# Weights split in the context half, odd tiles interpolated in another bank, and eleven blocks with an order of their own on each engine

## The chip, the cores and the metric

The kernel runs on one core of a Trainium2 chip (trn2). Its time is the device time of that core in microseconds; smaller is better. Four instruction queues matter here: TensorE (PE), VectorE (DVE), ScalarE (ACT) and GpSimd (POOL). Each runs its own list in order. They meet only in semaphores. SyncE (SP) issues most transfers.

## The reference, cut to what matters

Two layers, each a cross attention and a small expert network, over 2048 tokens of 256 numbers and a context of 1601 rows. The change lies in the second layer:

```python
x = x + _L1_xattn_ref(_layernorm(x), ctx_1024, ...)
x = x + _L1_ffn_ref(_layernorm(x), gate_W, expert_W, out_W)

# _L1_xattn_ref(char_emb = tokens, subword_emb = context)
char2sub = softmax(Q_char @ K_sub.T * scale) @ V_sub        # one row for each token
sub2char = softmax(Q_sub @ K_char.T * scale) @ V_char       # one row for each context row
sub2char = _interp_linear(sub2char, L_char)                 # 1601 rows stretched to 2048
gate = sigmoid(concat([char2sub, sub2char]) @ Wg.T + bg)
out = gate * char2sub + (1 - gate) * sub2char

# _L1_ffn_ref: eight logits, their softmax, p > 0.3 counted; what is left of the experts is two products
h = einsum('nd,ehd->neh', x, expert_W); final = einsum('neh,ne->nh', h, scale); out = final @ out_W.T
```

## The kernel before, in words

All of the second layer is one function, `cross_phase`. Its score blocks are numbered n = 0 to 111. Blocks 0 to 55 are the context half: groups 0 to 5 of context rows attend to the tokens and give `sub2char`. Group 5 has blocks 40 to 55; they are narrower in keys (one key tile each, three row tiles). Blocks 56 to 111 are the cross half: groups 6 to 13, seven blocks each, two token tiles per group, attending to the 1601 context rows. The last block of each group has one key tile, the others two.

A block n passes through the engines so: PE `score` (some blocks ahead), ACT `evacuate` (L2342), DVE `maximum` (L2693, L2696), then once per group the maxima are turned on PE (`max_turn`, L2093), reduced on DVE (`tops`, L2706), spread on ACT (`spread_max`, L2352) and turned back on PE (`spread_turn`, L2100). Then DVE `subtract` (L2717), ACT `exponent` (L2357) and `high` (L2364), DVE `low` (L2722), PE `weighted` (L2118 to L2120). High and low are the two float32r parts of a float32 number; each product is three matmuls (`mm3`, L43 to L45).

When a group closes, DVE `finish` (L2733, L2747) writes `c2s` for its two tiles, the even one u and the odd one v = u + 1. Each tile then goes through a closing chain over the blocks of the groups after it. In words, with lines: POOL `tents_of` makes the interpolation weights, PE `interpolate` (L2137, L2138) makes `sub2char` of the tile in a PSUM bank, ACT `copy` (L2399) keeps it in `inter`, POOL `mix` (L2599, L2600), PE `turn` (L2146), ACT `gate_high` (L2386), DVE `gate_low` (L2756), PE `gate`, DVE `bias` (L2763), ACT `squash` (L2390), DVE `move` (L2769, L2773) and `statistics` (L2779, L2782), POOL `inverse` (L2605 to L2609), ACT `normalise` (L2405), PE `x_turn` (L2166), `x_split` on ACT (L2376) and DVE (L2752), PE `first_products`, ACT `keep_first` (L2370), DVE and ACT `softly` and `soft_exponent` (L2797 to L2812, L2380), PE `second_product`, DVE `add` (L2820, L2825), SP store.

What sets the order is the loop `for n in range(NBLK)` on each engine: with b the block's place in its group (0 to 6), `closing_step`, `early_step`, `middle_step` and `late_step` hang one piece of the chain on each b. For the odd tile v, `interpolate(v)` stands at the end of b = 2 on PE, `copy(v)` at the start of b = 3 on ACT, and `turn(v)` on PE just behind `weighted` of b = 3. On ACT, `spread_max` of the next group stands at the end of b = 2, so ahead of `copy(v)`. Interpolation, turned tile and gate product share bank 0 (`jb`). After block 111 the rest of the chains of tiles 12 to 15 follows, in a list written by hand.

The closing weights (`late_weights`: expert 0, expert 1, Wg and the small gate matrix of the experts) are split into high and low by ACT (L2512) and DVE (L2936) at the ends of blocks 58, 59, 60 and 61.

## Time and profile before

| | |
|---|---|
| median of 3 runs | 1010.18 us (1009.96 to 1013.87) |
| the profiled execution, its own time | 1008.3 us |
| its span | 1006.4 us |
| PE busy | 940.8 us (93%) |
| DVE busy | 742.5 us (74%) |
| ACT busy | 584.8 us (58%) |
| POOL busy | 357.4 us (36%) |

The span runs from the first to the last instruction. Busy times are unions of instruction times. Matmuls overlap each other in a record, so PE reads as busy whenever it is fed. All times below are from the start of the span. On it the cross half's blocks run from about 746 us to 968 us, one group in some 28.5 us, and what remains of the closing chains runs from there to 1003.6 us.

### The profile page before, as it was taken

To read this page: it belongs to the slowest core of one execution; us is meant where nothing else is said; L and a number is where in the kernel's file an instruction comes from. 1 tells how busy PE (TensorE), PEld (TensorE's weight loads), DVE (VectorE), ACT (ScalarE), POOL (GpSimd) and SP (SyncE) were. 2 spreads that over 40 slices of the span, in tenths; PEclk is the share of its full clock that TensorE was granted. 3 is DMA by queue.
4 is the path that set the end of the run, shared out by engine and by line. 5 is a ranking of instruction groups with operands and counts; after the bars stand their busy time and mean duration, and the time that the engine had idled before them with its cause. 6 is when DMAs were issued, how large, how long until landed. Compare 5 with 4: busy or idle time off the path is not lost. (4 is left out here: it accounts for less than half of the span.)

```text
span 1006.4 us, 19300 instructions
## 1 busy us (share of the span) xinstructions
PE 940.8 (93%) x6934; PEld 885.3 (88%) x6934; DVE 742.5 (74%) x1704; ACT 584.8 (58%) x1243; POOL 357.4 (36%) x512
## 2 busy tenths in 40 slices
PE   8999999899899999999999999999996999999864
PEld 8899998588899999997788999999996989999764
DVE  7678777577687888865566677776588489898874
ACT  6356666432477777762345766665575466666431
POOL 4515555508334443315632000000026345544461
PEclk9999999999999999999999999999998999999987
DMA  8200000111588888824212000001000000000000
GB/s 239 84 1 1 1 1 1 42 44 63 185 262 265 266 259 253 262 95 129 63 42 85 1 1 2 1 2 43 1 22 2 1 12 22 20 14 23 21 22 21
DMA packets 50949, 72.38 MB, mean 72 GB/s; under 512 B 5489, under 2 KB 33777, under 8 KB 50865
## 3 DMA queue, kind: packets, MB, share of 16 engines
q1 hardware_dynamic: 45152, 55.81, 18.1%
q0 software_dynamic: 5024, 14.42, 4.2%
q8 instruction: 50, 0.82, 0.3%
q10 hardware_dynamic: 688, 1.05, 0.3%
q14 instruction: 35, 0.28, 0.1%
HBM read 59.34 MB, written 11.93 MB: 71 GB/s over the span
## 5 line engine op out<-in xcount | busy, mean ns | idle before, releaser
L2118 PE MATMUL wide<-V_hi,pt 128*128 128x258 f32 x400 | 117.7, 294 | 5.4 <-DVE pt L2722 5.4
L2120 PE MATMUL wide<-V_hi,pt 128*128 128x258 f32 x400 | 114.8, 287 | 0.0
L2119 PE MATMUL wide<-V_lo,pt 128*128 128x256 f32 x400 | 114.3, 286 | 0.0
L2118 PEld LDWEIGHTS wide<-V_hi,pt 128*128 128x128 f32 x400 | 77.3, 193 | 6.0 <-DVE pt L2722 5.8
L2579 POOL TENSOR_SCALAR V_hi<-rows 128x256 fp32r<-128x256 f32 (+1 forms) x9 | 8.9, 984 | 202.8 <-PE bank L2120 202.0
L2119 PEld LDWEIGHTS wide<-V_lo,pt 128*128 128x128 f32 x400 | 77.9, 195 | 0.2
L2120 PEld LDWEIGHTS wide<-V_hi,pt 128*128 128x128 f32 x400 | 77.5, 194 | 0.0
L43 PE MATMUL bank<-rx_hi,expert_w_hi 128*128 128x256 f32 x256 | 73.6, 287 | 1.6 <-PEq L1100 1.6
L45 PE MATMUL bank<-rx_hi,expert_w_lo 128*128 128x256 f32 x256 | 71.5, 279 | 0.0
L44 PE MATMUL bank<-rx_lo,expert_w_hi 128*128 128x256 f32 x256 | 71.5, 279 | 0.0
L503 POOL DMA_INDIRECT rxr<-token_rows,lists x39 | 56.8, 1457 | 27.6 <-issue 14.9
L43 PE MATMUL wide<-XT_hi,expert_w_hi 128*128 128x256 f32 (+1 forms) x216 | 63.8, 295 | 0.0
L44 PE MATMUL wide<-XT_lo,expert_w_hi 128*128 128x256 f32 (+1 forms) x216 | 62.3, 289 | 0.0
L45 PE MATMUL wide<-XT_hi,expert_w_lo 128*128 128x256 f32 (+1 forms) x216 | 62.3, 289 | 0.0
L514 DVE TENSOR_TENSOR expert_w_lo<-sraw,expert_w_hi 128x1024 fp32r<-128x1024 f32 x39 | 47.3, 1222 | 15.5 <-ACT expert_w_hi L510 15.4
L2696 DVE TENSOR_TENSOR rows<-rows,Fx 128x512 f32<-128x512 f32 (+2 forms) x60 | 40.7, 678 | 24.2 <-ACT Fx L2342 23.4
L1541 DVE TENSOR_TENSOR a0pt<-bank,a0pt 128x512 fp32r<-128x512 f32 x64 | 37.4, 584 | 28.0 <-ACT a0pt L1405 27.5
L1298 PE MATMUL bank<-a0pt,expert_w_hi 128*128 128x256 f32 x208 | 56.1, 300 | 1.4 <-issue 1.3
L43 PE MATMUL bank<-XT_hi,expert_w_hi 128*128 128x512 f32 x136 | 54.7, 402 | 1.5 <-PEq L1212 0.6
L43 PE MATMUL wide<-CT_hi,expert_w_hi 128*128 128x256 f32 (+1 forms) x192 | 55.2, 287 | 0.9 <-DVE XT_lo L2642 0.9
L45 PE MATMUL wide<-CT_hi,expert_w_lo 128*128 128x256 f32 (+1 forms) x192 | 54.8, 286 | 0.0
L44 PE MATMUL wide<-CT_lo,expert_w_hi 128*128 128x256 f32 (+1 forms) x192 | 54.8, 286 | 0.0
(527 smaller groups left out, 3639.6 us busy)
## 6 DMA issues: line engine op xcount, KB each, us to landing
sraw<-w1T SPq DMA_DIRECT2D x14, 512.0 KB, 4.6
sraw<-w3T SPq DMA_DIRECT2D x14, 512.0 KB, 4.9
sraw<-w2T SPq DMA_DIRECT2D x14, 512.0 KB, 5.0
raw_even<-w1T SPq DMA_DIRECT2D x11, 512.0 KB, 4.4
raw_even<-w3T SPq DMA_DIRECT2D x11, 512.0 KB, 5.0
raw_even<-w2T SPq DMA_DIRECT2D x11, 512.0 KB, 5.0
routed_results<-rys POOLq DMA_DIRECT2D x15, 256.0 KB, 4.5
X<-x SPq DMA_DIRECT2D x4, 512.0 KB, 6.6
```

The costliest lines, as they stand in the source:

```text
L43: pe.matmul(out, wh, xh, start=first, stop=False)
L44: pe.matmul(out, wh, xl, start=False, stop=False)
L45: return pe.matmul(out, wl, xh, start=False, stop=last)
L503: pool.indirect_dma_start(xr[:, j % 2, t, :], None, rows_in[:, :], bass.IndirectOffsetOnAxis(ap=lists[:, q:q + 1], axis=0))\
L514: dve.tensor_tensor(w_lo[:, par, piece(k)], raws[par][:, piece(k)], w_hi[:, par, piece(k)].bitcast(F32), ALU.subtract).then_inc(split_done ...
L1298: pe.matmul(ob[:, 0:2 * P], V_hi[:, k, :], both, start=k == 0, stop=False)
L1541: dve.tensor_tensor(weights(g, 1), transposed(g), weights(g, 0).bitcast(F32), ALU.subtract).then_inc(tlo, 1)
L2118: pe.matmul(dst[:, 0:D + 2], hi[:, x], v_hi(k), start=opens(n) and j == 0, stop=False)
L2119: pe.matmul(dst[:, 0:D], hi[:, x], v_lo(k), start=False, stop=False)
L2120: m = pe.matmul(dst[:, 0:D + 2], lo[:, x], v_hi(k), start=False, stop=closes(n) and k == keys_of(n)[-1])
L2579: pool.tensor_scalar(tent(i)[:, 0:n * P], d, 1.0, 0.0, ALU.add, ALU.max).then_inc(tent_done, 1)
L2696: dve.tensor_tensor(mx[:, 0:w], mx[:, 0:w], place(n), ALU.max).then_inc(maxed, 1)
```

## The change

Four things.

1. The closing weights are split at blocks 47, 48, 49 (expert 0, Wg, gate matrix) and 57 (expert 1), no longer at 58 to 61. Waits on `late_low` are renumbered.
2. Odd tiles are interpolated in bank 2 (`ib`), one block earlier: `interpolate(v)` at b = 1, `copy(v)` at b = 2.
3. POOL makes the tents four tiles ahead (before: two), and `inverse(i - 1)` comes behind `mix(i)`. Tokens 13 to 15 have places of their own and are fetched early. Several semaphores are split in two (`moved` into `scaled` and `moved`, `stat` into `stat` and `gathered`, `soft` into three).
4. The loops end at block 101 (`END_AT`). Blocks 101 to 111 and all that is left of tiles 9 to 15 follow as a written list for each engine. Tiles 13, 14 and 15 get banks of their own for gate and x work (`jb`, `xb`, `second_bank`), tile 15 its own gate inputs (`gin`), and tiles from 11 on two buffers `xn_of`.

```diff
+                LATE = [first[SG - 1] + 7, first[SG - 1] + 8, first[SG - 1] + 9, NSB + 1]
...
-                        if NSB + 2 <= n < NSB + 6:
-                            hi, lo, src = late_weights[n - NSB - 2]
+                        if n in LATE:
+                            hi, lo, src = late_weights[LATE.index(n)]
...
                 def jb(i):
-                    return score_bank[0] if i == LAST else banks[0]
+                    return score_bank[i - 13] if 13 <= i < LAST else banks[0]
 
                 def xb(i):
-                    return score_bank[1] if i == LAST else banks[1 + i % 2]
+                    return mb if i == 14 else banks[1] if i == LAST else banks[1 + i % 2]
+
+                def second_bank(i):
+                    return weighted_bank[i - 14] if i >= 14 else xb(i)
+
+                def ib(i):
+                    return jb(i) if i % 2 == 0 or i >= 13 else banks[2]
...
+                        elif i % 2 == 0:
+                            pe.wait_ge(biased, i)
+                        elif i > 4:
+                            pe.wait_ge(out_done, i - 3)
                         else:
-                            pe.wait_ge(biased, i)
+                            pe.wait_ge(finished, NC)
...
-                        if b == 2 and real(v):
+                        if b == 1 and real(v):
                             interpolate(v)
...
-                        if b == 3 and real(v):
+                        if b == 2 and real(v):
                             copy(v)
...
-                    tents_of(1)
-                    for i in range(NT):
+                    for i in range(1, 4):
+                        tents_of(i)
+                    for i in range(11):
                         mix(i)
-                        if real(i + 2):
-                            tents_of(i + 2)
-                        inverse(i)
+                        if i:
+                            inverse(i - 1)
+                        if i < 10:
+                            tents_of(i + 4)
...
-                    for n in range(NBLK):
+                    for n in range(END_AT):
...
+                    turn(11)
+                    weighted(END_AT)
+                    spread_turn(NG - 1)
+                    weighted(END_AT + 1)
+                    gate(11)
+                    weighted(END_AT + 2)
+                    first_products(9)
+                    weighted(END_AT + 3)
+                    interpolate(12)
+                    second_product(9)
+                    interpolate(13)
+                    x_turn(10)
+                    turn(12)
+                    weighted(END_AT + 4)
+                    turn(13)
+                    weighted(END_AT + 5)
+                    gate(12)
+                    weighted(END_AT + 6)
+                    first_products(10)
+                    weighted(END_AT + 7)
+                    gate(13)
+                    weighted(END_AT + 8)
+                    weighted(END_AT + 9)
+                    weighted(END_AT + 10)
+                    x_turn(11)
...
+                    gate(14)
+                    gate(15)
...
```

The lists of ACT, DVE and POOL are of the same kind. Three places show what moves.

First, DVE just behind the maxima of group 7 (L2706 is `tops`, L2936 the low part of a closing weight, L2696 a maximum, L2717 the subtractions for group 7, L2733 the first step of `finish` for tile 0). Before:

```order
L2706 TENSOR_REDUCE top<-bank 128x2
L2936 TENSOR_TENSOR expert_w_lo<-sraw,expert_w_hi 128x512
L2693 COPY rows<-Fx 128x512
L2722 TENSOR_TENSOR pt<-Fx,pt 128x256
L2936 TENSOR_TENSOR expert_w_lo<-sraw,expert_w_hi 128x1024
L2696 TENSOR_TENSOR rows<-rows,Fx 128x512
L2717 TENSOR_TENSOR Fx<-Fx,bank 128x512 x4
L2936 TENSOR_TENSOR expert_w_lo<-rt_raw,expert_w_hi 128x2x8
L2733 RECIPROCAL inverse_sum<-wide 128x1
```

The same place on DVE now (line numbers of the changed kernel: L2838 is `tops`, L2828 the maximum, L2849 the subtractions, L2865 the first step of `finish`):

```order
L2838 TENSOR_REDUCE top<-bank 128x2
L2825 COPY rows<-Fx 128x512
L2854 TENSOR_TENSOR pt<-Fx,pt 128x256
L2828 TENSOR_TENSOR rows<-rows,Fx 128x512
L2849 TENSOR_TENSOR Fx<-Fx,bank 128x512 x4
L2865 RECIPROCAL inverse_sum<-wide 128x1
```

Three splits are gone from between them; the fourth stays some rows ahead.

Second, PE at b = 2 of a group in the cross half, between the last score and `weighted` of b = 3 (L2166 is `x_turn`, L2137 and L2138 `interpolate` of the odd tile, L2093 `max_turn`, L2118 `weighted`). Before:

```order
L45 MATMUL wide<-XT_hi,expert_w_lo 128x256
L2166 MATMUL bank<-ident,sraw 128x128 x2
L2137 MATMUL bank<-CT_hi,V_lo 128x256
L2138 MATMUL bank<-CT_lo,V_lo 128x256
L2093 MATMUL bank<-ident,rows 128x128 x2
L2118 MATMUL wide<-V_hi,pt 128x258
```

Now (L2201 is `x_turn`, L2115 `max_turn`, L2140 `weighted`):

```order
L45 MATMUL wide<-XT_hi,expert_w_lo 128x256
L2201 MATMUL bank<-ident,sraw 128x128 x2
L2115 MATMUL bank<-ident,rows 128x128 x2
L2140 MATMUL wide<-V_hi,pt 128x258
```

The interpolation has gone up by one block, behind the even tile's gate product.

Third, DVE from the last `tops` on, where the written list begins. Before (L2752 is `x_split` of tile 9, L2756 `gate_low`, L2769 and L2773 `move`, L2717 `subtract` for group 13, L2722 `low`):

```order
L2706 TENSOR_REDUCE top<-bank 128x2
L2752 TENSOR_TENSOR XT_lo<-bank,XT_hi 128x2x128
L2722 TENSOR_TENSOR pt<-X,pt 128x512
L2756 TENSOR_TENSOR expert_w_lo<-bank,expert_w_hi 128x512
L2769 SCALAR_TENSOR_TENSOR sraw<-sraw 128x256
L2773 SCALAR_TENSOR_TENSOR X<-sraw,X 128x256
L2779 BN_STATS stats<-X 128x6
L2782 BN_AGGR MV<-stats 128x2
L2717 TENSOR_TENSOR Fx<-Fx,bank 128x512 x3
```

Now (L2884 is `x_split`, L2889 `gate_low`, L2902 and L2906 `move`, L2849 `subtract`, L2854 `low`, L2896 `bias`):

```order
L2838 TENSOR_REDUCE top<-bank 128x2
L2902 SCALAR_TENSOR_TENSOR sraw<-sraw 128x256
L2854 TENSOR_TENSOR pt<-X,pt 128x512
L2906 SCALAR_TENSOR_TENSOR X<-sraw,X 128x256
L2889 TENSOR_TENSOR expert_w_lo<-bank,expert_w_hi 128x512
L2849 TENSOR_TENSOR Fx<-Fx,bank 128x512
L2884 TENSOR_TENSOR XT_lo<-bank,XT_hi 128x2x128
L2849 TENSOR_TENSOR Fx<-Fx,bank 128x512
L2912 BN_STATS stats<-X 128x6
L2849 TENSOR_TENSOR Fx<-Fx,bank 128x512
L2896 TENSOR_TENSOR sraw<-bank,rows 128x256
```

Work of several tiles now alternates with the block work, one instruction of each.

## Rows read from the trace of the kernel before

**Rows 1.** The page's head and one of its groups (count, busy us, mean ns).

```profile
span 1006.4 us, 19300 instructions
...
L2696 DVE TENSOR_TENSOR rows<-rows,Fx 128x512 f32<-128x512 f32 (+2 forms) x60 | 40.7, 678 | 24.2 <-ACT Fx L2342 23.4
```

**Rows 2.** Windows: stretch, its length, then PE, PEld, DVE, ACT, POOL, PEclk.

```profile
710.00:740.00 30.00, 29.76 (x238) 29.36 (x237) 16.24 (x43) 16.50 (x44) 0.00 (x0) 0.94 0.00 1
777.80:784.10 6.30, 6.28 (x31) 6.29 (x32) 3.15 (x5) 0.72 (x3) 5.01 (x5) 0.53 0.01 3
878.90:907.40 28.50, 27.21 (x227) 26.86 (x227) 24.71 (x61) 18.43 (x47) 13.95 (x20) 1.00 0.06 19
934.80:967.60 32.80, 27.40 (x209) 26.50 (x210) 25.77 (x69) 17.51 (x44) 18.27 (x28) 0.95 0.08 25
951.50:968.00 16.50, 14.63 (x120) 14.01 (x118) 12.72 (x38) 7.83 (x21) 11.67 (x17) 1.00 0.08 25
967.60:1003.60 36.00, 19.78 (x94) 16.91 (x92) 19.94 (x66) 7.43 (x24) 10.03 (x18) 0.72 0.06 19
934.80:1006.40 71.60, 47.18 (x300) 43.42 (x300) 45.71 (x135) 24.95 (x67) 28.30 (x45) 0.83 0.07 23
```

**Rows 3.** Waits from 829 to 944 us: total us, times, longest.

```profile
DVE XT_lo L2752 <- ACT XT_hi L2376: 5.2, 4, 1.3
PE bank L2146 <- ACT sraw L2399: 4.8, 4, 1.2
DVE sraw L2763 <- PE bank L45: 4.0, 4, 1.1
```

**Rows 4.** Timeline of DVE, ACT and PE at b = 3, 905 to 908 us.

```profile
905.82 0.41 DVE L2706 TENSOR_REDUCE top<-bank 128x2 f32<-128x256 f32 x1
906.27 0.69 ACT L2352 ACTIVATE rows<-ident,top 128x128 f32<-128x128 f32 x2 [1.58 <-DVE top L2706]
906.87 0.36 ACT L2399 ACTIVATE sraw<-bank 128x256 f32<-128x256 f32 x1
907.54 0.42 DVE L2752 TENSOR_TENSOR XT_lo<-bank,XT_hi 128x256 fp32r<-128x256 f32 x1 [1.30 <-ACT XT_hi L2376]
907.38 0.41 PE L2146 MATMUL bank<-ident,sraw 128*128 128x128 f32 x2 [1.20 <-ACT sraw L2399]
```

**Rows 5.** Timeline of PE at b = 3 of group 8.

```profile
822.35 0.30 PE L2146 MATMUL bank<-ident,sraw 128*128 128x128 f32 x1 [0.44 <-ACT sraw L2399]
```

**Rows 6.** Timeline around the closing weights, DVE, ACT and PE, 767 to 778 us.

```profile
767.11 0.42 DVE L2722 TENSOR_TENSOR pt<-Fx,pt 128x256 fp32r<-128x256 f32 x1
768.70 0.47 ACT L2342 ACTIVATE Fx<-wide,t_c 128x256 f32<-128x256 f32 x1
769.06 1.06 ACT L2512 ACTIVATE expert_w_hi<-sraw 128x1024 fp32r<-128x1024 f32 x1
770.15 1.23 DVE L2936 TENSOR_TENSOR expert_w_lo<-sraw,expert_w_hi 128x1024 fp32r<-128x1024 f32 x1 [2.63 <-ACT expert_w_hi L2512]
775.56 1.00 DVE L2696 TENSOR_TENSOR rows<-rows,X 128x512 f32<-128x512 f32 x1
777.82 0.58 PE L2118 MATMUL wide<-V_hi,pt 128*128 128x258 f32 x1 [4.07 <-DVE pt L2722]
```

**Rows 7.** Timeline of DVE and PE, 755 to 764 us.

```profile
755.54 2.88 DVE L2722 TENSOR_TENSOR pt<-Fx,pt 128x512 fp32r<-128x512 f32 x1
763.73 0.69 PE L2093 MATMUL bank<-ident,rows 128*128 128x128 f32 x2 [3.84 <-DVE rows L2700]
```

**Rows 8.** Waits from 932 us to the end.

```profile
PE bank L43 <- DVE XT_lo L2752: 8.7, 4, 4.1
...
DVE sraw L2763 <- PE wide L45: 6.2, 1, 6.2
...
PE bank L2166 <- ACT sraw L2405: 5.8, 3, 3.7
```

**Rows 9.** Transfer issue on SP and its time to landing; the last DVE instruction.

```profile
699.34 0.51 SPq L2000 DMA_DIRECT2D sraw<-folded_weights  x1
...
sraw<-folded_weights SPq DMA_DIRECT2D x1, 512.0 KB, 5.0
...
1003.08 0.48 DVE L2825 SCALAR_TENSOR_TENSOR rows<-wide,sc,rows 128x256 f32<-128x256 f32 x1
```

More of the change, by code:

```diff
@@ L2013, in _ @@
                         sp.wait_ge(stored, 16 * (i + 1))
-                        if i + 4 < NT:
+                        if i <= 8:
                             token_back(i + 4)
+                        if i == 7:
+                            sp.wait_ge(low_done, first[NG - 2] + 1)
+                            for k in range(13, NT):
+                                token_back(k)
                 @blk.tensor
@@ new lines, in _ @@
+                    high(END_AT + 3)
+                    squash(11)
+                    high(END_AT + 4)
+                    high(END_AT + 5)
+                    keep_first(9)
+                    exponent(END_AT + 6)
+                    normalise(10)
+                    copy(12)
+                    x_split(10)
+                    copy(13)
+                    high(END_AT + 6)
+                    gate_high(12)
+                    exponent(END_AT + 7)
+                    soft_exponent(9)
@@ new lines, in _ @@
+                    copy(14)
+                    copy(15)
+                    keep_first(11)
+                    gate_high(14)
+                    normalise(12)
+                    gate_high(15)
+                    soft_exponent(11)
+                    x_split(12)
+                    squash(14)
+                    squash(15)
+                    keep_first(12)
+                    normalise(13)
+                    x_split(13)
+                    soft_exponent(12)
+                    normalise(14)
@@ new lines, in _ @@
+                    subtract(END_AT + 5)
+                    statistics(10, 0)
+                    subtract(END_AT + 6)
+                    bias(11)
+                    low(END_AT + 3)
+                    subtract(END_AT + 7)
+                    statistics(10, 1)
+                    move(11, 0)
+                    low(END_AT + 4)
+                    finish(NG - 2, 0)
+                    move(11, 1)
+                    finish(NG - 2, 1)
+                    softly(9, 0)
+                    statistics(11, 0)
@@ new lines, in _ @@
+                    low(END_AT + 5)
+                    subtract(END_AT + 8)
+                    softly(9, 1)
+                    gate_low(12)
+                    x_split(10)
+                    subtract(END_AT + 9)
+                    statistics(11, 1)
+                    low(END_AT + 6)
+                    subtract(END_AT + 10)
+                    soft_end(9)
+                    low(END_AT + 7)
+                    add(9, 0)
+                    gate_low(13)
+                    low(END_AT + 8)
@@ new lines, in _ @@
+                    bias(12)
+                    low(END_AT + 9)
+                    softly(10, 0)
+                    add(9, 1)
+                    softly(10, 1)
+                    move(12, 0)
+                    bias(13)
+                    move(12, 1)
+                    low(END_AT + 10)
+                    statistics(12, 0)
+                    soft_end(10)
+                    statistics(12, 1)
+                    move(13, 0)
+                    finish(NG - 1, 0)
+                    x_split(11)
@@ new lines, in _ @@
+                    finish(NG - 1, 1)
+                    add(10, 0)
+                    move(13, 1)
+                    add(10, 1)
+                    softly(11, 0)
+                    statistics(13, 0)
+                    softly(11, 1)
+                    gate_low(14)
+                    statistics(13, 1)
+                    gate_low(15)
+                    soft_end(11)
+                    bias(14)
+                    add(11, 0)
+                    x_split(12)
+                    move(14, 0)
@@ new lines, in _ @@
+                    bias(15)
+                    move(14, 1)
+                    add(11, 1)
+                    statistics(14, 0)
+                    softly(12, 0)
+                    move(15, 0)
+                    statistics(14, 1)
+                    move(15, 1)
+                    softly(12, 1)
+                    x_split(13)
+                    statistics(15, 0)
+                    soft_end(12)
+                    statistics(15, 1)
+                    softly(13, 0)
+                    add(12, 0)
@@ new lines, in _ @@
+                    softly(13, 1)
+                    x_split(14)
+                    add(12, 1)
+                    soft_end(13)
+                    softly(14, 0)
+                    softly(14, 1)
+                    x_split(15)
+                    add(13, 0)
+                    soft_end(14)
+                    softly(15, 0)
+                    softly(15, 1)
+                    add(14, 0)
+                    add(13, 1)
+                    soft_end(15)
+                    add(14, 1)
@@ L2974, in build @@
+                    add(15, 0)
+                    add(15, 1)
         folded_dram = nc.dram_tensor("folded_weights", (P, 2 * DC * D), F32, kind="Internal").ap()
```

265 lines of the change are left out of this document (148 added, 117 removed).

## The prediction, written before the changed kernel was run

> **What bounds the kernel now.** I read the windows first, then the waits, then the timeline at each wait of more than a microsecond that PE had. Over the whole span PE is the busy engine, so the first question is where it is not fed. The stretch from 710 to 740 us, the end of the context half, shows PE busy for 29.76 of 30 us while DVE and ACT have some 13.5 us free each [rows 2]. One group of the cross half takes 28.5 us, in which PE works 27.21 and DVE 24.71 [rows 2]. So both are close to their limit there, and PE has about 1.3 us to give. From 934.8 us the picture turns: up to 967.6 us PE works 27.4 of 32.8, and behind it 19.78 of 36, with DVE at 19.94 of 36 and the clock at 0.72 of full speed [rows 2]. That last stretch is bound by no engine but by hand-overs: PE waits 8.7 us for the low parts of tiles and 5.8 us for normalised tiles, DVE 6.2 us at one stroke for a gate product [rows 8]. So there are three places, and the change touches each.
>
> **Closing weights.** Before, four splits stand on DVE at 58 to 61. The third is the dear one. DVE is through at 767.53 (767.11 + 0.42) and has to wait 2.63 us for ACT, which has itself waited for the evacuation at 768.70 to 769.17. Then it works 1.23 us, and goes on at 771.3 [rows 6]. What it goes on with is a maximum that needs only that evacuation, so without the split it starts at 769.2: 2.1 us earlier. PE's 4.07 us wait at 777.82 ends when DVE's low part is there, and all between is in DVE's order, so PE gets about 2.0 us of it. The first of the four (expert 0) is replaced by expert 1 one block earlier, in the same jammed stretch. So the 3.84 us wait for `max_turn` [rows 7] stays; I take nothing there. Behind the 4.07 us wait the clock stood at 0.53 for 6.3 us: 31 matmuls in 6.28 us, 0.20 us each, against 120 in 14.63 us, 0.12 each, at clock 1.00 [rows 2]. With half the wait the low clock may not come; that is worth up to 31 x 0.08 = 2.5 us. I leave it out of the sum and put it in the range. At the new place the three splits cost ACT and DVE some 2 us each over three blocks, where each has about 13.5 of 30 us free; PE does not see it as long as the low parts stay more than a block ahead. If that cover failed, it would cost the length of one split, 1.2 us. The largest transfer that ACT must wait for there is issued at 699.34 and takes 5.0 us [rows 9], so it has landed before the stretch from 710 us on, in which blocks 47 to 49 lie. **Term: -2.0 us, bounds -4.5 and +1.**
>
> **Odd tiles.** At b = 3 PE wants to turn the odd tile and waits 1.20 us for `copy` (L2399), four times between 829 and 944, 4.8 us [rows 3]. The copy itself is 0.36 us, but on ACT it stands behind `spread_max`, which waits for DVE's `tops` at 905.82 + 0.41 [rows 4]. Moved to b = 2 the copy is ahead of it. PE's wait goes whole. DVE's wait of 1.30 us for `XT_hi` shrinks by the copy's start-to-start, about 0.26 us, since `spread_max` is still in front. What is late next? DVE's other waits are 1.1 us a group for PE's gate product [rows 3]. PE coming 1.2 us earlier and DVE 0.26 earlier nearly fills these. So the group's length goes to PE's own work, 27.2 us, or a little more: I take 1.1 of 1.2. The new wait that could replace it is `x_turn` at b = 2 for `copy`, and the copy for the interpolation that now ends half a microsecond behind the gate product. ACT has 10 us free in a group, and evacuates a later score in that block anyway, so nothing. The group before them waits only 0.44 us [rows 5]; DVE is full there. Sum: 0.4 + 1.0 for the next interval + 3 x 1.1. **Term: -4.7 us, bounds -5.3 and -1 (if DVE is the real limit and only its 0.26 counts).**
>
> **The last eleven blocks.** From 934.8 (the last `tops`) to the end DVE has 45.71 us of work [rows 2], and its last instruction ends at 1003.56 [rows 9]: 68.8 us, a third of it idle. The new lists hold the same arithmetic. So 45.7 us is the floor of this stretch as long as DVE is the busiest, and PE's work, 300 records, is 36.6 us at 0.122 us each. I walked through the lists with the durations of the trace. Nearly every closing piece finds its input ready, since two to five tiles are in work at once. The gate products of 14 and 15 follow one another, where before the second waited for the first tile's whole chain. To place the result between 45.7 and 68.8 I use the group stage. There DVE does 24.71 of 28.5, and 24.71 of 27.3 when the term above holds, 9.5% idle. At that density 45.7 becomes 50.5. The last three tiles can't be as dense: their chains run bare at the end, and PE will fall to the lower clock there, as in the 0.72 stretch. Behind block 111 PE has 98 matmuls and some 18 transposes left: 14 us at 0.122, and 24 us at the 0.21 of the 0.72 stretch (19.78 us for 94). The latter is as much as DVE has. I add 2.5 us and take 53. **Term: 53 - 68.8 = -15.8 us, bounds -18.5 (density of the group stage) and -6 (half of the idle stays in the blocks, and the low clock holds to the end).**
>
> The levels of the clock are 1.2 and 2.4 GHz; 0.53 is nearly all at the lower, after PE had waited 4.07 us. The Trainium skill ("TensorE: Matmul & The Clock Gate", section "What's actually happening") says that the clock knows only these two and that an idle spell brings the lower one. The trace agrees in the matmul pitch, 0.20 against 0.12 us; by that rule a denser end would stay at the higher level, and the third term would be nearer its lower bound.
>
> **The sum.** -2.0 - 4.7 - 15.8 = -22.5 us. The profiled execution took 1008.3 us, 1.9 more than its span and 1.9 less than the median. So 985.8 for a profile and **987.7** for the median.
>
> **Rivals.**
> The end pays by half. For it: hand-overs between PE, ACT and DVE remain in each tile's chain, and the clock of 0.72. Against: DVE has other tiles' work in front of most. Third term -8: 995.5 us.
>
> POOL takes DVE's time. POOL now makes two more sets of tents right behind the row splits, from about 766 to 778 us, where it was idle. In such company DVE's low part at 755.54 took 2.88 us where its like takes 0.68, and the maximum at 775.56 took 1.00 against a mean of 0.678 [rows 7, 6, 1]. Against: from 777.8 to 784.1 POOL works 5.01 us on tents and DVE's five instructions there take 3.15 us [rows 2], as elsewhere. Four instructions at 0.3 to 1 us more take 1.3 to 4 us: 990. The Trainium skill ("SBUF — State Buffer", section "SBUF: two separate sides") says that a DVE instruction with two SBUF inputs and a GpSimd instruction exclude each other for their whole length. The 2.88 us agree, the 5.01 us row does not show it.
>
> The end's order pays nothing; only the first two terms: 1003.5 us.
>
> Slower. Single mechanism: on PE the blocks 102 to 111 now queue behind closing pieces (three gate products, two first products, a second product, two turns). If each of these eight has to wait for ACT and DVE like its fellows in the old end (8.7/4 and 5.8/3, about 2 us [rows 8]), that is 16 us, and if the blocks' 120 matmuls fall to the lower clock for it, 120 x 0.08 = 9.6 us more. The end is then 53 + 25.6 = 78.6 us instead of 68.8, and with -6.7 from the first two terms the whole is 3 us slower, 1013 us. At 3 us each it is 1021 us. It decides from 1.6 us each on, and is told from no change from 2.2 us on. Against: in the group stage the same pieces stand between the same blocks and PE waits 1.3 us in 28.5.
>
> **How the numbers follow.** As forecast 0.62, own range 981 to 993; by half 0.20; POOL 0.07; only the first two terms 0.05; no difference 0.03; slower 0.03. A measurement of this kernel can tell about 0.5%, 5 us, from no change. All cases up to the fourth are faster by more: 0.94. Same 0.035, slower 0.025. The range 980 to 999 leaves out the last three (0.11) and the far ends of the first two.
>
> **What would show it.** Term one: the 2.63 us wait of DVE is gone, PE's 4.07 us wait is near 2 us, PE's busy share at the new blocks is unchanged. Term two: the turn at b = 3 no longer waits, groups are 27.2 to 27.5 us long. Term three: from the last `tops` to DVE's last instruction 50 to 56 us, block 111 closes some 7 us earlier relative to it, and no PE wait is over 3 us. The prediction is wrong if PE waits inside the eleven blocks for closing pieces, if the clock in the last 25 us is near 0.5, or if DVE's instructions grow under POOL's.

## The result, and the profile after

The changed kernel takes 977.7 us (977.44 to 978.32, 4 runs). The kernel before takes 1010.07 us beside it (1009.68 to 1013.87, 4 runs). The ratio is 0.967, with a 95% interval of 0.965 to 0.970. So the kernel is faster by 3.3%, 2.3 us beyond the fast edge of the range. The profiled execution took 977.88 us, with a span of 976.1 us.

The page's head after, and the group of maxima (count, busy us, mean ns), which answer to [rows 1]:

```profile
span 976.1 us, 19295 instructions
...
L2828 DVE TENSOR_TENSOR rows<-rows,Fx 128x512 f32<-128x512 f32 (+2 forms) x60 | 42.1, 702 | 24.5 <-ACT Fx L2414 23.6
```

Windows after, with the columns of [rows 2]: the new place of the splits, the stretch behind the first context block of the closing stage, one group, the end up to the last `weighted`, the end behind it, and the end as a whole:

```profile
710.00:740.00 30.00, 29.18 (x230) 28.57 (x229) 17.25 (x44) 17.08 (x45) 0.00 (x0) 0.94 0.00 1
777.60:783.90 6.30, 6.25 (x53) 6.25 (x54) 5.72 (x9) 4.64 (x10) 5.48 (x6) 1.00 0.01 3
872.00:899.00 27.00, 27.00 (x230) 27.00 (x230) 23.98 (x62) 18.12 (x45) 15.42 (x21) 1.00 0.07 20
926.00:950.40 24.40, 22.71 (x188) 22.01 (x186) 21.67 (x63) 14.80 (x36) 14.21 (x21) 1.00 0.06 17
950.40:972.10 21.70, 15.91 (x116) 13.75 (x114) 20.05 (x75) 9.86 (x30) 6.70 (x15) 0.99 0.07 25
926.00:976.10 50.10, 38.62 (x301) 35.76 (x299) 41.75 (x137) 24.66 (x66) 20.91 (x35) 0.96 0.08 25
```

PE now has no gap in a group. The clock stays up through the end, where [rows 2] had 0.72. PE's waits from 926 us on (total, times, longest) answer to [rows 8]:

```profile
PE bank L2201 <- ACT sraw L2484: 1.2, 2, 0.7
PE bank L43 <- DVE XT_lo L2884: 1.1, 2, 0.9
PE bank L2201 <- ACT rows L2484: 1.0, 1, 1.0
PE bank L2122 <- ACT rows L2424: 0.8, 1, 0.8
PE bank L43 <- DVE expert_w_lo L2889: 0.5, 1, 0.5
```

The 8.7 and the 5.8 us of [rows 8] have shrunk to 1.1 and 2.2 us (1.2 and 1.0). The timeline after, in the order of time: two rows of the new place of the splits, the wait that was 4.07 us in [rows 6], the first odd turn that waited 0.44 us in [rows 5], DVE's last three instructions, and between them the issue of the last two stores.

```profile
730.90 1.21 DVE L3071 TENSOR_TENSOR expert_w_lo<-sraw,expert_w_hi 128x1024 fp32r<-128x1024 f32 x1
...
733.78 0.84 ACT L2414 ACTIVATE Fx<-wide,t_c 128x256 f32<-128x256 f32 x2 [2.44 <-DVE t_c L2813]
...
777.65 0.39 PE L2140 MATMUL wide<-V_hi,pt 128*128 128x258 f32 x1 [1.84 <-DVE pt L2854]
...
818.92 0.60 PE L2176 MATMUL bank<-ident,sraw 128*128 128x128 f32 x4
...
970.73 0.48 DVE L2960 SCALAR_TENSOR_TENSOR Fx<-wide,sc,Fx 128x256 f32<-128x256 f32 x1
971.13 0.47 DVE L2955 SCALAR_TENSOR_TENSOR Fx<-sraw,sc,Fx 128x256 f32<-128x256 f32 x1
...
971.48 2.07 SPq L2030 DMA_DIRECT2D out<-Fx  x2
...
971.64 0.48 DVE L2960 SCALAR_TENSOR_TENSOR Fx<-wide,sc,Fx 128x256 f32<-128x256 f32 x1
```

To compare kernels I cut each trace at five marks: PE's start of the turn of the second context max (M), the start of the turn of tile 3 (T), the start of the last `tops` (S), the end of DVE's last instruction (V), and the span. The last three columns are differences of these. The names are those in the headings below.

| kernel | M | T | S | V | span | M to T | T to S | S to V |
|---|---|---|---|---|---|---|---|---|
| before | 763.73 | 822.35 | 934.35 | 1003.56 | 1006.4 | 58.6 | 112.0 | 69.2 |
| after | 764.52 | 818.92 | 926.12 | 972.12 | 976.1 | 54.4 | 107.2 | 46.0 |
| late_only | 768.79 | 824.14 | 936.18 | 1005.20 | 1008.1 | 55.4 | 112.0 | 69.0 |
| late_and_odd | 767.04 | 821.51 | 929.43 | 996.86 | 999.7 | 54.5 | 107.9 | 67.4 |
| old_lists | 764.65 | 818.56 | 925.77 | 993.18 | 996.1 | 53.9 | 107.2 | 67.4 |
| tents_back | 766.99 | 821.25 | 929.15 | 986.67 | 990.6 | 54.3 | 107.9 | 57.5 |
| late_back | 765.58 | 822.51 | 929.67 | 975.97 | 979.9 | 56.9 | 107.2 | 46.3 |
| odd_back | 764.31 | 819.08 | 929.23 | 977.79 | 981.7 | 54.8 | 110.2 | 48.6 |
| stores_free | 765.00 | 819.41 | 926.58 | 972.89 | 975.8 | 54.4 | 107.2 | 46.3 |
| stores_early | 765.39 | 819.42 | 926.62 | 972.94 | 975.8 | 54.0 | 107.2 | 46.3 |
| dve_twice | 768.75 | 823.16 | 930.37 | 977.61 | 981.6 | 54.4 | 107.2 | 47.2 |
| act_twice | 767.22 | 820.18 | 927.39 | 974.12 | 978.1 | 53.0 | 107.2 | 46.7 |
| pe_twice | 767.41 | 821.40 | 928.59 | 975.86 | 979.8 | 54.0 | 107.2 | 47.3 |

Each row is one profiled execution. The last two columns repeat within 0.4 us where nothing in their stretch differs. M to T also depends on how long PE ran at the lower clock in it, which the windows from M to T show, with the columns of [rows 2], here of before, after and late_back:

```profile
763.73:822.35 58.62, 52.54 (x400) 51.56 (x401) 39.92 (x83) 34.19 (x79) 24.03 (x29) 0.92 0.01 3
764.52:818.92 54.40, 50.93 (x400) 50.13 (x401) 39.18 (x80) 32.45 (x76) 34.54 (x41) 0.95 0.01 3
765.58:822.51 56.93, 52.47 (x400) 51.68 (x401) 40.00 (x83) 34.00 (x79) 36.95 (x41) 0.92 0.01 3
```

The same 400 matmuls keep PE busy for 50.9 to 52.5 us at mean clocks of 0.95 and 0.92. In act_twice the clock is 0.97 and PE's busy time 49.96 us, which is 1.0 of the 1.4 us by which its M to T is shorter than that of the changed kernel. M itself wanders by up to 5 us; what wanders is shown under the hardware.

The 30.3 us that the span lost are these: 0.8 more up to M, 4.2 less from M to T, 4.8 less from T to S, 23.2 less from S to V, and 1.1 more behind V (4.0 against 2.8 us).

### The profile page after: what moved, and what is told of

Read it like the earlier page. It is cut to its first block and busy times, and to the rows that moved or that the text cites. A ratio compares the mean times of both kernels' runs of the same rounds, so it can differ in the third digit from the quotient of the medians.

```text
span 976.1 us, 19295 instructions
## 1 busy us (share of the span) xinstructions
PE 929.8 (95%) x6934; PEld 876.2 (90%) x6934; DVE 736.2 (75%) x1704; ACT 583.0 (60%) x1243; POOL 359.0 (37%) x512
## 5 line engine op out<-in xcount | busy, mean ns | idle before, releaser
L2140 PE MATMUL wide<-V_hi,pt 128*128 128x258 f32 x400 | 116.8, 292 | 3.2 <-DVE pt L2854 3.2
L2696 POOL TENSOR_SCALAR V_hi<-rows 128x256 fp32r<-128x256 f32 (+1 forms) x9 | 9.7, 1081 | 203.6 <-PE bank L2142 202.9
L2140 PEld LDWEIGHTS wide<-V_hi,pt 128*128 128x128 f32 x400 | 76.3, 191 | 3.8 <-DVE pt L2854 3.6
L2142 PEld LDWEIGHTS wide<-V_hi,pt 128*128 128x128 f32 x400 | 76.5, 191 | 0.0
L503 POOL DMA_INDIRECT rxr<-token_rows,lists x39 | 56.9, 1458 | 27.6 <-issue 15.5
L2828 DVE TENSOR_TENSOR rows<-rows,Fx 128x512 f32<-128x512 f32 (+2 forms) x60 | 42.1, 702 | 24.5 <-ACT Fx L2414 23.6
L514 DVE TENSOR_TENSOR expert_w_lo<-sraw,expert_w_hi 128x1024 fp32r<-128x1024 f32 x39 | 47.4, 1223 | 15.8 <-ACT expert_w_hi L510 15.7
L1541 DVE TENSOR_TENSOR a0pt<-bank,a0pt 128x512 fp32r<-128x512 f32 x64 | 37.4, 584 | 27.9 <-ACT a0pt L1405 27.5
```

Of the source, the lines that this page charges most:

```text
L503: pool.indirect_dma_start(xr[:, j % 2, t, :], None, rows_in[:, :], bass.IndirectOffsetOnAxis(ap=lists[:, q:q + 1], axis=0))\
L514: dve.tensor_tensor(w_lo[:, par, piece(k)], raws[par][:, piece(k)], w_hi[:, par, piece(k)].bitcast(F32), ALU.subtract).then_inc(split_done ...
L1541: dve.tensor_tensor(weights(g, 1), transposed(g), weights(g, 0).bitcast(F32), ALU.subtract).then_inc(tlo, 1)
L2140: pe.matmul(dst[:, 0:D + 2], hi[:, x], v_hi(k), start=opens(n) and j == 0, stop=False)
L2142: m = pe.matmul(dst[:, 0:D + 2], lo[:, x], v_hi(k), start=False, stop=closes(n) and k == keys_of(n)[-1])
L2828: dve.tensor_tensor(mx[:, 0:w], mx[:, 0:w], place(n), ALU.max).then_inc(maxed, 1)
```

## Experiments

### The early splits alone (late_only)

The kernel before with the four splits at their new blocks and the waits renumbered, nothing else:

```diff
+                LATE = [first[SG - 1] + 7, first[SG - 1] + 8, first[SG - 1] + 9, NSB + 1]
...
-                        if NSB + 2 <= n < NSB + 6:
+                        if n in LATE:
```

> The kernel before with one part of the change: the closing weights split at blocks 47, 48, 49 and 57. Theory A, read from the trace after: the move saves 3.6 us between 764 and 794 us (the wait of 4.07 us before block 63 falls to 1.8, and the clock stays at the upper level behind it) and costs 0.8 us at blocks 47 to 49, so -2.8 us: about 1007.3 us. Rival B, my forecast's term: only the wait shrinks and the clock still falls, -2.0 us, 1008.1. Rival C: in the changed kernel it was the moved tents and the earlier odd copy that did this, and the weights alone give nothing or cost the 0.8 us: 1010 to 1011.

Measured 1008.67 us (1005.37 to 1009.87, 10 runs) against 1009.57 (1008.38 to 1013.6, 13 runs), ratio 0.998 (0.997 to 1.000). Too small for the medians to size. The trace sizes it: M to T is 3.3 us shorter (55.35 against 58.62), everything behind T as before. Of the 3.3, PE waits 2.1 us less, and 1.2 us is busy time that the higher mean clock saves (51.38 us at 0.94, against 52.54 at 0.92). The gain is near theory A's 3.6, but the clock did not stay at the upper level here: behind the wait, now 1.91 us, the 6.3 us from 780.7 have a mean of 0.73 (40 matmuls). What it paid ahead of M can't be read from this run, since its M is also shifted by the clock (below).

### Early splits and odd tiles, old end (late_and_odd)

> The kernel before with two parts: closing weights at 47, 48, 49, 57, and the odd tiles interpolated in bank 2, one block earlier. POOL's order and the end are those of before. Theory A: PE's wait for the copy at b = 3 is all that made a group longer than PE's work; groups fall from 28.4 to 27.0 to 27.2 us, 5 to 6 us in all on top of the first part: 1001 to 1002.5 us. Rival B: the groups get to 27.0 only with POOL's new order too (mix ahead of inverse, tents four ahead), and without it DVE stays the limit at 28.1: 1006. The end, from the last maxima's reduction to the last DVE instruction, stays at 69 us by both.

The edit adds `ib` with bank 2 and moves `interpolate(v)` to b = 1 and `copy(v)` to b = 2; loops and lists stay. Measured 1000.72 us (999.87 to 1001.52, 4 runs), ratio 0.991 (0.989 to 0.993). Over the run before it (one profile each) M to T loses 0.9 us, T to S 4.1, S to V 1.6: 6.6 us for the odd tiles. Theory A holds, but for the end, which both theories had kept at 69 us: it is 1.6 us shorter.

### The changed kernel with the old order of the end (old_lists)

Loops run to block 111 again and the old lists follow, while the own banks of tiles 13 to 15 and the tents four ahead stay:

```diff
-                    for n in range(END_AT):
+                    for n in range(NBLK):
...
-                    turn(11)
-                    weighted(END_AT)
-                    spread_turn(NG - 1)
...
+                    turn(LAST - 1)
+                    second_product(LAST - 3)
+                    interpolate(LAST)
```

> The changed kernel with the loops run to block 111 and the old lists behind them; the own banks and buffers of tiles 11 to 15, the semaphores and POOL's early tents stay. It tells the order of the last eleven blocks from the places. Theory A: the order does it; with the old order the second gate product still waits for the first tile's chain, the clock falls again behind block 111, and the end is 62 to 69 us long instead of 46: 994 to 1001 us. Rival B: own banks, own gate inputs and the second xn buffer take the waits away in any order: end of 50 us, 982 us.

Measured 998.14 us (997.69 to 1001.85), ratio 0.990 (0.987 to 0.992). S to V is 67.4 us, that of late_and_odd, so theory A holds. Banks and early tents alone give the end nothing. The waits from 926 us on are of the old kind, in sum longer than in [rows 8] (total, times, longest):

```profile
PEld bank L43 <- DVE XT_lo L2803: 14.2, 7, 4.3
PE bank L43 <- DVE XT_lo L2803: 12.4, 7, 4.1
...
DVE sraw L2815 <- PE bank L45: 6.2, 1, 6.2
```

### The changed kernel with the tents two ahead (tents_back)

```diff
-                    for i in range(1, 4):
-                        tents_of(i)
+                    tents_of(1)
                     for i in range(11):
                         mix(i)
-                        if i:
-                            inverse(i - 1)
-                        if i < 10:
-                            tents_of(i + 4)
+                        tents_of(i + 2)
+                        inverse(i)
```

The written end of POOL follows the same old order. The edit moves `inverse` back too, so it does not separate that from the tents.

> The changed kernel with POOL's order of before: tents two tiles ahead, inverse(i) behind them, so that POOL works 28 us instead of 21 us in the end. In the trace after, DVE's busy time in the end is 41.9 us against 45.7 before. Theory A: of these 3.9 us about 1.3 are instructions that POOL's work had made longer (the small ones, L2938 and L2940: 0.31 and 0.24 us each before, 0.23 and 0.17 after), the rest is that instructions back to back overlap by 0.07 us each in the record; so 979 us and the small ones long again. Rival B: POOL's work took all 3.9 us: 981.5 us. Rival C: the tents of tiles 12 to 15 come too late for PE now, and PE waits for them: 983 us or more, with waits for POOL on PE's interpolations.

Measured 992.11 us (991.7 to 996.16), ratio 0.984 (0.981 to 0.987): 14.4 us of the gain are gone, 11.5 of them in S to V. The timeline shows where, with POOL's tent just ahead of each wait:

```profile
941.65 0.65 POOL L2696 TENSOR_SCALAR V_hi<-rows 128x128 fp32r<-128x128 f32 x1
942.35 0.39 PE L2165 MATMUL wide<-CT_hi,V_hi 128*128 128x256 f32 x1 [4.06 <-POOL V_hi L2696]
...
963.48 1.07 POOL L2696 TENSOR_SCALAR V_lo<-rows 128x256 fp32r<-128x256 f32 x1
964.61 0.58 PE L2165 MATMUL bank<-CT_hi,V_lo 128*128 128x256 f32 x1 [4.78 <-POOL V_lo L2696]
```

In the old order POOL makes a tile's tents behind another tile's `mix` or `inverse`, which waits for a chain. PE waits 8.8 us for the tents, and engines behind it wait too. This is rival C. Theory A's short instructions did not grow: from S to V `pr` and `over` take 231 and 170 ns on average, 232 and 171 in the changed kernel, 309 and 240 before. So the new lists need POOL's new order, the tents ahead: without it they give 9.9 us (67.4 to 57.5), without the lists it gives none, together 21.4. I had listed this edit in the change and priced it only as a danger (DVE beside POOL).

### The splits back (late_back), the odd tiles back (odd_back)

Each undoes one part of the changed kernel. First the places of the splits:

```diff
-                LATE = [first[SG - 1] + 7, first[SG - 1] + 8, first[SG - 1] + 9, NSB + 1]
+                LATE = [NSB + 2, NSB + 3, NSB + 4, NSB + 5]
```

> The kernel after, but the four closing weights are split between tiles 1 and 5 of the closing stage again, as before; all else as after. Theory A (the splits delay the first turns of the tail, wherever the rest of the gain comes from): the run of the kernel before with the early splits alone lost 3.3 us between the second context max and the turn of tile 1, and paid 0.5 to 0.8 us of it back ahead of that max; here the same in reverse, so about 980.2 us (979.5 to 981), with a wait of TensorE near 4 us ahead of the first context block of the closing stage, a granted clock near 0.5 behind it, and an end (from the last tops to the last VectorE instruction) still of 46 us. Rival B (with odd tiles in a bank of their own and the written end the delay is soaked up by slack that was not there before): 977.7 us within 0.7, same landmarks from turn 3 on. Rival C (the splits between the tiles now collide with the new copies of the odd tiles on VectorE, which are made one block earlier): over 982 us.

Measured 981.26 us (978.94 to 982.81, 5 runs), ratio 0.971 (0.969 to 0.973), 3.6 us above the changed kernel; the intervals of the ratios just touch. M to T is 2.5 us longer, of which 1.5 is PE's busy time at the lower mean clock and 1.0 waiting (the windows under the table). T to S is that of the changed kernel and S to V within 0.3 us of it. PE's wait is back in part, and PE's busy time at the blocks that the splits left is back whole (windows and timeline of this run):

```profile
710.00:740.00 30.00, 29.76 (x237) 29.35 (x237) 16.66 (x45) 15.63 (x41) 0.00 (x0) 0.94 0.01 1
777.60:784.00 6.40, 4.30 (x36) 4.30 (x37) 5.35 (x9) 5.78 (x13) 6.06 (x7) 1.00 0.01 3
```

```profile
779.70 0.39 PE L2140 MATMUL wide<-V_hi,pt 128*128 128x258 f32 x1 [2.84 <-DVE pt L2854]
```

29.76 against 29.18 us is the price of the early splits: 0.6 us. The expected wait near 4 us with a clock near 0.5 behind it did not come: the wait was 2.84 us, and behind it the clock was 1.00.

Then the odd tiles up to 11, in bank 0 and a block later:

```diff
-                    return jb(i) if i % 2 == 0 or i >= 13 else banks[2]
+                    return jb(i)
...
-                        if b == 1 and real(v):
+                        if b == 2 and real(v):
                             interpolate(v)
...
-                        if b == 2 and real(v):
+                        if b == 3 and real(v):
                             copy(v)
```

> The kernel after, but the odd tiles up to 11 are interpolated in the shared bank again, two blocks into their group, and copied a block later, as before; closing weights and written end as after. Theory A (the bank costs about 1.3 us in each of the groups, as 28.4 against 27.05 us showed): five to six groups, so 984.5 us (983 to 986), groups of 28.4 us again, end of 46 us. Rival B (the late odd tile also reaches into the written end, whose first steps take tiles 10 and 11): 987 to 990 us, with the end over 48 us. Rival C (nothing, the gain of the run with both first parts having come from the copies alone): under 980 us.

Measured 984.76 us (983.26 to 986.25, 5 runs), ratio 0.975 (0.973 to 0.977), 7.1 us above the changed kernel; in its profile 5.6. The total is that of theory A. Groups lose 3.0 us (110.15 against 107.20 for T to S), less than it had. The end loses 2.6, as rival B had it: tile 11's turn stands right behind the late copy, which ends at 930.63. The timeline of this run:

```profile
930.74 0.69 PE L2172 MATMUL bank<-ident,sraw 128*128 128x128 f32 x4 [2.94 <-issue]
```

### Two attempts at a faster version (stores_free, stores_early)

SP no longer waits for each store to land from tile 9 on:

```diff
-                        sp.wait_ge(stored, 16 * (i + 1))
+                        if i <= 8 or i == LAST:
+                            sp.wait_ge(stored, 16 * (i + 1))
```

> The kernel after, but the queue that stores tiles no longer waits for each store's landing before it issues the next one, from tile 9 on (it waits once, at the end). In the kernel after 4.0 us lie between the last VectorE instruction and the end of the span, with the store of tile 15 issued only when that of tile 14 had landed; before it was 2.8 us. Theory A (two landings in series): 976.4 us (975.9 to 976.9), with 2.5 to 3.0 us behind the last VectorE instruction. Rival B (the end of the span is the landing of the last store and its own latency covers the wait): 977.7 us within 0.4.

Measured 977.58 us (976.17 to 979.36, 5 runs), ratio 0.968 (0.966 to 0.970). The trace agrees with theory A, 2.9 us behind V instead of 4.0, though the median did not move. The two last stores now issue in 1.25 us (timeline of this run), where the changed kernel needed 2.07.

```profile
972.01 1.25 SPq L2030 DMA_DIRECT2D out<-Fx  x2
...
972.41 0.48 DVE L2961 SCALAR_TENSOR_TENSOR Fx<-wide,sc,Fx 128x256 f32<-128x256 f32 x1
```

The median can't show 1.1 us beside a spread of 3. With the first three splits two blocks earlier besides:

```diff
-                LATE = [first[SG - 1] + 7, first[SG - 1] + 8, first[SG - 1] + 9, NSB + 1]
+                LATE = [first[SG - 1] + 5, first[SG - 1] + 6, first[SG - 1] + 7, NSB + 1]
```

> As the run without the waits between stores, and the first three of the four closing weights are split two context steps earlier (45 to 47 instead of 47 to 49), where VectorE's row shows it half idle. The splits at 47 to 49 pushed the context max by 0.8 us, by a wait of ScalarE for a copy of VectorE that stood behind a split of 1.2 us. Theory A (that wait goes): 975.8 us, 0.6 to 0.8 below the run without the waits between stores. Rival B (any place in the context half costs the same, since VectorE's copies feed ScalarE at every step): same as that run within 0.3. Rival C (at 45 the raw weights have not landed, or the split meets the context max): 0.5 us or more above it.

Measured 977.23 us (976.21 to 978.28, 5 runs), ratio 0.967 (0.966 to 0.969). PE's busy time at the place rises from 29.18 to 29.56 us (window of this run), so 0.4 of the 0.6 us come back. Neither the medians nor the intervals tell this version from the changed kernel; inconclusive for the whole, right for the place.

```profile
710.00:740.00 30.00, 29.56 (x236) 29.15 (x235) 18.09 (x47) 16.57 (x45) 0.00 (x0) 0.94 0.01 1
```

### Extra work on one engine at a time (dve_twice, act_twice, pe_twice)

Each adds work to the end of the changed kernel, whose results go to an unused place or are written again: DVE's statistics of tiles 10 to 15 twice; two short ACT copies ahead of each `keep_first` from tile 10 on; the transposes of tiles 12 to 15 twice.

```diff
+                            if i >= 10:
+                                dve.bn_stats(out=spare[:, 6 * (i - 10):6 * (i - 9)], in_=token(i))
```

> The kernel after, with VectorE's statistics of tiles 10 to 15 taken twice, the first time into an unused place: six more instructions of 0.416 us in the end, 2.5 us (2.0 if neighbours overlap in the record as the others do). Theory A (VectorE, busy for 41.9 of the 50.2 us from the last tops to the end of the span, sets the length of the written end): the end grows by most of it, 1.8 to 2.5 us, so 48 us from tops to the last VectorE instruction, and about 979.8 us. Rival B (the end is bound by chains over several engines, whose gaps take an extra instruction): under 1.2 us more. Compared with the two runs in which ScalarE and TensorE get the same amount of extra work.

```diff
+                        for j in range(2 if i >= 10 else 0):
+                            o = (2 * (i - 10) + j) * 36
+                            act.activation(spare[:, o:o + 36], xb(i)[:, 0:36], ACT.Copy)
```

> The kernel after, with two short extra copies of 36 columns on ScalarE ahead of each keep_first of tiles 10 to 15, twelve instructions of about 0.2 us (as its 8-column exponents take): 2.4 us more of ScalarE's work in the end, on the way of the tile's last chain. Theory A (ScalarE, busy for 24.7 of 50.2 us, has room): under 1 us more, 977.7 to 978.6 us. Rival B (chains bound the end, and each instruction on one counts whatever its engine): 1.8 to 2.4 us more, as much as the run with the extra statistics.

```diff
-                        for t, src in enumerate((c2s, inter)):
+                        for t, src in enumerate((c2s, inter) * (2 if i >= 12 else 1)):
+                            t %= 2
```

> The kernel after, with the four transposes of each turn of tiles 12 to 15 issued twice: sixteen more of about 0.15 us, 2.4 us more of TensorE's work in the end. TensorE is busy for 38.7 of the 50.2 us of the end. Theory A (VectorE alone sets it): under 1 us more. Rival B (TensorE sets the first half of the end, where the weighted products of three tiles run, and VectorE the second): 0.5 to 1.5 us for the turns that fall ahead of the last weighted product (tiles 12 and 13), nothing for the others. Rival C (TensorE sets it throughout): 2.4 us, 980.1 us.

Medians: 981.24 us (979.26 to 983.37), 979.59 (978.09 to 979.88) and 981.54 (978.5 to 984.31), against 1009.09 before, ratios 0.971, 0.970 and 0.972, each within 0.002. They hold the wandering of M, so I go by S to V in one profile each. It is 46.0 to 46.3 us in the four kernels with the unchanged end, so a difference of 0.3 us is no effect. What the extra work cost its engine, in the groups of each run (count, busy us, mean ns), DVE first:

```profile
L2914 DVE BATCH_NORM_STATS2 spare<-X 128x6 f32<-128x256 f32 x3 | 1.2, 415 | 0.0
L2914 DVE BATCH_NORM_STATS2 spare<-Fx 128x6 f32<-128x256 f32 x2 | 0.8, 414 | 0.0
L2914 DVE BATCH_NORM_STATS2 spare<-rows 128x6 f32<-128x256 f32 x1 | 0.4, 418 | 0.0
```

ACT:

```profile
L2445 ACT ACTIVATE spare<-bank 128x36 f32<-128x36 f32 x12 | 1.7, 196 | 1.8 <-PE bank L45 1.8
```

PE, where the two groups of transposes had 1.2 us each in the changed kernel:

```profile
L2177 PE MATMUL bank<-ident,sraw 128*128 128x128 f32 x16 | 2.1, 274 | 0.0
L2177 PE MATMUL wide<-ident,sraw 128*128 128x128 f32 x16 | 2.1, 272 | 0.0
```

DVE's 2.4 us lengthen the end by about 1.0 (47.2 against 46.2), ACT's 1.7 by 0.5, PE's 1.8 by 1.1. No engine's extra work counts whole; that of DVE and PE counts in part, and ACT's 0.5 is little more than the spread. My theory that DVE alone sets the length falls (1.8 to 2.5 expected), and so do the ones by which ACT's or PE's extra work counts whole (1.8 to 2.4, and 2.4). For PE 0.9 of it falls ahead of the last `weighted` (from S to there 25.1 us against 24.3), as rival B had it. I read this as an end bound by chains over several engines that are nearly full at different times: PE in the first half, DVE in the second (22.71 of 24.40 and 20.05 of 21.70 us in the windows above). No run takes work away from an engine, which would test it from the other side.

## Why the prediction was right or wrong

**Place and sign** were right: all three terms came, none on the other side. The sum was 7.8 us short in the profile (22.5 against 30.3), and 1.9 us more were added on top that were not there.

**Closing weights**, -2.0 forecast: -3.3 alone and -2.5 in the changed kernel from M to T, against 0.6 paid at the new place, so -2.7 and -1.9. That the sum term is so near is partly luck. The cover that I named there was nearly whole: a 1.21 us split on DVE stands ahead of `t_c`, ACT's evacuation waits 2.44 us for it, and PE loses half a microsecond. PE's 4.07 us wait fell to 1.84, as forecast, and the low clock behind it went (53 matmuls in 6.3 us, where [rows 2] have 31). I had left that out of the sum. The split of M to T into waiting and busy time sizes both: the waits gave 2.1 us alone and 1.0 in the changed kernel, the clock 1.2 and 1.5. So the wait that I had put at 2.0 is worth half of that in the changed kernel, and the clock that I had put at nothing makes up for it.

**Odd tiles**, -4.7 forecast: -6.6 forward and -5.9 in reverse, beyond the bound of -5.3. The last three groups came to 27.0 us (the windows have 27.00 of 27.00 us busy; `tops` starts at 845.14, 872.14, 899.30 and 926.12), just under the 27.2 to 27.5 that I looked for, because I took PE's 27.21 us of [rows 2] as the least that a group can take. With the holes gone the same work is 27.0 us. The step "3 x 1.1" was a little small and the end was missing from it: tile 11's turn opens the end, and 1.6 to 2.6 us come there.

**The last eleven blocks**, -15.8 forecast, -23.2 measured, of which 1.6 belong to the odd tiles. This is the term that was mis-sized, in two of its steps. The first is "So 45.7 us is the floor of this stretch". The busy time of one order is no floor for another order. From S to V the timelines hold the same 136 instructions of DVE before and after. Their durations add up to 49.6 us before and 48.3 after, and the time in which at least one of them runs, the busy time of the windows, is 46.1 before and 41.6 after. So 1.3 of the 4.5 us are shorter instructions, and 3.2 are overlap of neighbours in the record. A row that reads what the row before it wrote mostly begins some 0.04 us behind that row's end. One that doesn't mostly begins 0.08 us ahead of it. Before, the moves and statistics of one tile stood in a row:

```profile
937.81 0.42 DVE L2769 SCALAR_TENSOR_TENSOR sraw<-sraw 128x256 f32<-128x256 f32 x1
938.26 0.42 DVE L2773 SCALAR_TENSOR_TENSOR X<-sraw,X 128x256 f32<-128x256 f32 x1
938.72 0.43 DVE L2779 BATCH_NORM_STATS2 stats<-X 128x6 f32<-128x256 f32 x1
```

Now work of several tiles alternates (970.73 plus 0.48 is 971.21, and the next row starts at 971.13). Of the 135 rows behind the first, 42 begin ahead of their predecessor's end before, and 85 after. That it is the order and not the idle time shows in two runs, both with an end much longer than 46 us. From S to V, tents_back has the new order and a busy time of 42.41 us on DVE, though a quarter of its end is idle; old_lists has the old order and 46.18:

```profile
929.15:986.67 57.52, 42.69 (x303) 39.84 (x301) 42.41 (x137) 24.85 (x66) 28.61 (x45) 0.91 0.05 17
925.77:993.18 67.41, 44.92 (x300) 41.67 (x298) 46.18 (x137) 24.32 (x66) 18.94 (x35) 0.85 0.05 17
```

With 41.7 us (21.67 and 20.05 in the windows) at the density that I had taken, 9.5% idle, the end is 46.1 us, and it measured 46.0. That the density was hit so closely is partly luck: the runs with extra work show that the length does not follow DVE's work. The second is "I add 2.5 us": PE stayed at clock 1.00 and 0.99 in both halves, and none of its waits there is over 1.0 us. The two are 4.5 and 2.5 us, together with 0.4 for the start of the stretch the whole 7.4 that this term was short.

**What was left out.** POOL's new order stands in no term, and the end needs it (tents_back). The end behind V grew by 1.1 us, since two stores in series now close it. And "1.9 less than the median" was no property of the kernel: the profile of before had caught an execution without the slow stretch at 248 us, shown below.

**The rivals.** The end paid by more than half. POOL beside DVE as a danger of the new tents did not come. The mean maximum did grow from 678 to 702 ns, 1.4 us over all 60. But it is 700 ns in late_only, where POOL's order is the old one, and 680 in late_back, where it is the new one: it follows the place of the splits. The 2.88 us that a low part took in [rows 7], beside POOL's row splits, now falls to a maximum. The Trainium skill ("SBUF — State Buffer", section "SBUF: two separate sides") would have a DVE instruction with two SBUF inputs and a GpSimd one that reads SBUF exclude each other. The window at 777.6 shows DVE busy for 5.72 and POOL for 5.48 of 6.3 us, but busy time holds such waits too, and the rows agree with the page:

```profile
778.16 1.19 POOL L2717 TENSOR_TENSOR X<-X,sraw 128x256 f32<-128x256 f32 x1
778.75 1.15 DVE L2828 TENSOR_TENSOR rows<-rows,X 128x512 f32<-128x512 f32 x1
...
780.42 0.68 DVE L2854 TENSOR_TENSOR pt<-Fx,pt 128x512 fp32r<-128x512 f32 x1
780.57 1.04 POOL L2689 TENSOR_SCALAR rows<-rows 128x128 f32<-128x128 f32 x1
```

The maximum starts inside POOL's row, takes 1.15 us in place of 0.68, and ends 0.55 us behind it. POOL's 1.04 us starts inside DVE's row, takes 0.65 in tents_back at 940.22, and ends 0.51 us behind DVE's. The slower case needed 1.6 us of wait at each of eight pieces; PE's listed waits in the end add up to 4.6 us.

**What stays open:** how much of the 21.4 us each single place in the new lists is worth, which of tents and `inverse` POOL's order needs, and what sets how long PE stays at the lower clock between M and T.

## What to carry to other kernels

When a stretch is to be reordered, its busy time is no floor. On DVE here neighbours that did not depend on each other overlapped in the record by about 0.08 us and dependent ones did not, and an order that alternates tiles took 3.2 us of the 46.1 off its busy time. Follow every producer of the new order, also the engine that seems to have time: here POOL's old order, with the tents two tiles later, cost 11.5 of the 21.4 us. And compare kernels by stretches between marks rather than by totals when the total wanders by more than the effect.

## What was not expected of the hardware

A stretch far ahead of every edit runs at either level of the clock, from one execution to the next. Windows of the same 10 us in the kernel before, with the columns of [rows 2]:

```profile
248.00:258.00 10.00, 10.00 (x65) 9.00 (x66) 5.66 (x10) 3.13 (x4) 0.67 (x1) 1.00 0.18 52
```

in act_twice:

```profile
248.00:258.00 10.00, 10.00 (x60) 9.37 (x60) 4.49 (x9) 2.90 (x4) 0.00 (x0) 0.83 0.07 24
```

and in dve_twice:

```profile
248.00:258.00 10.00, 10.00 (x48) 9.19 (x49) 3.09 (x6) 1.56 (x3) 0.00 (x0) 0.66 0.01 2
```

PE reads as fed for all of the 10 us in each, and gets 65, 60 or 48 matmuls done: at 1.00 all of it runs at 2.4 GHz, at 0.83 and 0.66 a part at 1.2 GHz. The longest wait of PE in the 35 us around it in dve_twice is 0.8 us. M stands at 763.7 us in the first, 767.2 in the second, 768.8 in the third. Of the thirteen profiles six have 1.00 from 200 to 300 us, and their M is 763.7 to 765.4; seven have 0.97 or 0.98, and M at 765.6 to 768.8. The 765.6 is late_back, the only one with no lower clock from 470 to 530 us either (1.00 there, 0.97 or 0.94 in the others). The medians of one kernel spread by 3 to 5 us; that this is where most of it comes from is likely, but there is one profile of each kernel, so it is not shown. The Trainium skill ("TensorE: Matmul & The Clock Gate", section "What's actually happening") says of the start of a kernel that the point at which the level changes differs from run to run; these traces show the like in the middle of one.

The clock did not follow the length of a wait alone either: the 4.07 us wait of [rows 6] was followed by 0.53, waits of 1.84 and 2.84 us at the same place by 1.00, and one of 1.91 us (late_only) by 0.73.
